# A two-layer graph network on one core: the preparation and the first layer's products in one block, instead of one after the other

## The chip, the cores and the metric

The kernel runs on one NeuronCore of a Trainium2 chip. The metric is the device time of one execution in microseconds; less is better. Engines are named as the profile names them: PE is TensorE, DVE is VectorE, ACT is ScalarE, POOL is GpSimd, SP is SyncE, which here only issues DMAs.

## The reference, cut to what matters

1,250 nodes with 768 features, 40,000 edges sorted by destination. A graph attention block (four heads of 512, then one of 768), then a graph convolution block. All matrix products are float32; the kernel makes them from two parts (hi and lo) of each operand, in three products.

```python
h = jnp.maximum(_layernorm(x, axis=-1), 0.0)
x = x + _L0_gnn_ref(h, edge_index, ...)          # two attention layers
h = jnp.maximum(_layernorm(x, axis=-1), 0.0)
x = x + _L1_gnn_ref(h, ..., edge_index)          # two graph convolutions

def _gat_layer(x, src, dst, W, a_src, a_dst, bias, concat):
    h = (x @ W).reshape(N, H, C)                 # W1: 768 x (4*512)
    al_s = jnp.einsum('nhc,hc->nh', h, a_src)
    al_d = jnp.einsum('nhc,hc->nh', h, a_dst)
    e = jax.nn.leaky_relu(al_s[src] + al_d[dst], NEG_SLOPE)
    ...softmax over the edges of a destination, weighted sum, + bias
```

## The kernel before, in words

Rows stand in `T` = 10 tiles of 128 nodes. Each block of the program (`nc.Block()`) gives every engine a queue of its own, in the order in which the code is written; engines wait for each other only through semaphores, and at the end of a block all of them meet at a barrier. There is no scheduler. `build` calls `front`, `first_layer` and `second_half`; the change touches the first two.

`front` (lines 202 to 442) does two things. **The rows:** SP loads ten tiles of `x` into `xr`; DVE takes the statistics of all ten (`row_stats`, lines 169 and 170), ACT takes the root of all ten variances at once (line 302), DVE makes `rstd` and `nmr` (lines 175 to 179 and 432); POOL normalizes tile by tile (line 293), PE turns each tile by six transposes into the PSUM tile `p_x` (line 345), ACT writes `xT_hi` with the relu (line 305) and DVE `xT_lo` (line 439). **The edges:** DVE and PE turn the sorted edges into `parts_of`, from which later the matrix of edge counts is made: `edges_in`, `chunk_windows`, `edge_keys`, `window_bounds`, `spread_chunks`, `window_parts` on DVE, `transpose_edges`, `transpose_spans`, `window_rows`, `pick_chunks` on PE. These stand between the tiles, by the two dictionaries `between`.

`first_layer` then makes the products with W1. Head after head (order 1, 2, 3, 0), tile after tile, `tile(n)` is 18 matmuls of 512 columns (six slices of the features, three hi and lo products each, line 1137); n runs to `FIRST` = 30, and ten more follow for head 0. ACT copies each product to `stage` (line 705, two slots) and SP stores it in `h_scratch` (line 641). A `stage` slot is written again only when its store has landed (`spilled`), and `tile(n)` waits until `stage` holds tile n-2. Beside this, DVE builds one-hot rows for 80 windows (`hot`, line 808, seven slots), PE counts each window with six small matmuls (line 1150) and ACT writes three windows at a time to `counts` (line 695). `windows_after(n)` gives three windows after each of the tiles 0 to 26. DVE also reduces W1 with the attention vectors (`attention_column`, line 861; four after each of the first three tiles of a head, by `columns(n)`, counted by the semaphore `v_done`). At each change of head the one copy of W1's slice, `w_st`, is split into `w_hi` (ACT, line 690) and `w_lo` (DVE, line 802).

The next head's weights overwrite `w_st`, so SP loads them only after the last use of the old ones. That wait stands in SP's queue ahead of the store of tile 6:

```python
if n in (6, 16, 22):
    j = {6: 1, 16: 2, 22: 3}[n]
    sp.wait_ge(v_done, 2 * KD * j)
    sp.wait_ge(wlo_done, KD * j)
    load_weights(sp, j)
sp.wait_ge(h_out, n + 1)
sp.dma_start(h_scratch[ORDER[i], :, n % T, :], stage[:, n % 2, :]).then_inc(spilled[n % 2], 16)
```

After tile 28 comes one more count with a dynamic number of rounds (`extra_chunks` on DVE, `count_extra` on PE; one round with these edges), which needs all windows in `counts`.

Of the kernel before, what the change touches and what calls it, by code (L numbers as in the profile page):

```python
# [83 lines left out]
class Memory:  # L84

    def __init__(self, nc, keep):
# [46 lines left out]
        self.abc = late("abc", [P, 2, HID], fp32)  # L133


def build(nc, x, src, dst, W1, as1, ad1, b1, W2, as2, ad2, b2, G1, c1, G2, c2, out):
    keep = ExitStack()
    with keep:
# [7 lines left out]
        def load_weights(sp, i):  # L146
            h = ORDER[i]
            for a, vec in enumerate((as1, ad1)):
                sp.dma_start(mem.abc[:, a, :], vec[h:h + 1, :].to_broadcast([P, HID])).then_inc(a_in, 16)
            sp.dma_start(mem.w_st[:, :, :], W1.rearrange("(k p) n -> p k n", p=P)[:, :, h * HID:(h + 1) * HID]).then_inc(w_in, 16)  # L150

        with ExitStack() as st:
            front(nc, st, mem, x, src, dst, load_weights, tile_in)
        with ExitStack() as st:
            first_layer(nc, st, mem, W2, b1, as2, ad2, h_scratch, w_in, a_in, load_weights, tile_in)
# [44 lines left out]


def front(nc, st, mem, x, src, dst, load_weights, tile_in):
    pb, sem = makers(nc, st)
    sb = Area(nc, mem.at_w, mem.at_late)
    ident, ones, pick, xT = mem.ident, mem.ones, mem.pick, mem.xT
    codes, parts_of, place, low, key = mem.codes, mem.parts_of, mem.place, mem.low, mem.key
    until, reach, total = mem.until, mem.reach, mem.total
    xr = Area(nc, mem.at_weights, mem.at_weights + T * D * 4)("xr", [P, T, D], fp32)
    stats = sb("stats", [P, T, 2, 6], fp32)
    mv = sb("mv", [P, T, 2], fp32)  # L210
    ve, root, rstd, nmr, tmp = (sb(n, [P, T], fp32) for n in ("ve", "root", "rstd", "nmr", "tmp"))
    e_i = sb("e_i", [EP, 2, EJ, EC], i32)
    e_f = sb("e_f", [EP, 2, EJ, EC], f32r)
    s_i = sb("s_i", [EC, NW * FIX], i32)
    s_hi = sb("s_hi", [EC, NW * FIX], i32)
    s_lo = sb("s_lo", [EC, NW * FIX], i32)
    d_f = sb("d_f", [EC, NW * FIX], fp32)
    sc = Area(nc, mem.at_hs, mem.at_weights)
    spread = [sc(f"spread{j}", [EP, NW, FIX], f32r) for j in range(EJ)]
    steps = sc("steps", [EP, EJ, FIX], i32)  # L220
    steps_f = sc("steps_f", [EP, EJ, FIX], fp32)
    base = sc("base", [EC, NW, FIX], i32)
    base_f = sc("base_f", [EC, NW, FIX], fp32)
    w_i = sc("w_i", [EP, 2, NW], i32)
    w_f = sc("w_f", [EP, 2, NW], fp32)
    c_i = sc("c_i", [EP, 2, EJ], i32)
    c_f = sc("c_f", [EP, 2, EJ], fp32)
    dmm = sc("dmm", [EP, 2, EJ], fp32)
    ov = sc("ov", [EP, 2, EJ, NW], fp32)
    met = sc("met", [EP, 2, EJ, NW], fp32)  # L230
    cand = sc("cand", [EP, 2, NW], fp32)
    far = sc("far", [NW, 2], fp32)
    wc = sc("wc", [NW, 3], fp32)
    tri = sc("tri", [NW, NW], fp32)
    p_x = [pb("p_x0", [P, 8, P]), pb("p_x1", [P, 8, P])]
    p_e = pb("p_e", [EC, 2, 512])
    p_w = pb("p_w", [NW, 2, EP])
    p_r = pb("p_r", [P, 3, NW])
    e_in = sem("e_in")
    made = sem("made")  # L240
    v_step = sem("v_step")
    pad_zero = sem("pad_zero")
    roots = sem("roots")
    var_done = sem("var_done")
    norm_ready = sem("norm_ready")
    h_done = sem("h_done")
    xt_done = sem("xt_done")
    hi_done = sem("hi_done")
    lo_done = sem("lo_done")
    ef_ready = sem("ef_ready")  # L250
    et_done = sem("et_done")
    spread_ready = sem("spread_ready")
    picked = sem("picked")
    red_ready = sem("red_ready")
    wt_done = sem("wt_done")
    wc_ready = sem("wc_ready")
    wr_done = sem("wr_done")

    with nc.Block() as block:
        @block.sync  # L260
        def _(sp):
            for t in range(T):
                if t == T - 1:
                    sp.wait_ge(pad_zero, 1)
                sp.dma_start(xr[0:rows_of(t), t, :], x[t * P:t * P + rows_of(t), :]).then_inc(tile_in[t], 16)
            load_weights(sp, 0)

        @block.gpsimd
        def _(pool_):
            nc.gpsimd.memset(ident[:, :], 0.0).then_inc(made, 1)  # L270
            nc.gpsimd.memset(tri[:, :], 1.0).then_inc(made, 1)
            nc.gpsimd.memset(ones[:, :].bitcast(fp32), 1.0).then_inc(made, 1)
            nc.gpsimd.memset(pick[:, :].bitcast(fp32), 0.0).then_inc(made, 1)
            for a in range(2):
                nc.gpsimd.iota(w_i[:, a, :], pattern=[[WD, NW]], base=a * (WD - 1), channel_multiplier=0).then_inc(made, 1)
            nc.gpsimd.iota(c_i[:, 0, :], pattern=[[1, EJ]], base=1, channel_multiplier=EJ).then_inc(made, 1)
            nc.gpsimd.iota(c_i[:, 1, :], pattern=[[-1, EJ]], base=NCH, channel_multiplier=-EJ).then_inc(made, 1)
            nc.gpsimd.iota(steps[:, :, :], pattern=[[1, EJ], [-1, FIX]], base=0, channel_multiplier=EJ).then_inc(made, 1)
            nc.gpsimd.iota(base[:, :, :], pattern=[[-WK, NW], [0, FIX]], base=OFFSET, channel_multiplier=0).then_inc(made, 1)
            pool_.wait_ge(made, 10)  # L280
            nc.gpsimd.affine_select(out=ident[:, :], in_=ident[:, :], compare_op=ALU.not_equal, fill=1.0,
                                    base=0, pattern=[[-1, P]], channel_multiplier=1).then_inc(made, 1)
            nc.gpsimd.affine_select(out=tri[:, :], in_=tri[:, :], compare_op=ALU.is_ge, fill=0.0,
                                    base=0, pattern=[[1, NW]], channel_multiplier=-1).then_inc(made, 1)
# [1700 lines left out]
```

## Time and profile before

| what | us |
|---|---|
| three runs: median, lowest, highest | 1232.4, 1225.87, 1234.49 |
| the profiled execution: its own time | 1236.01 |
| its span | 1234.1 |
| PE, DVE, ACT busy in the span | 1135.5, 848.9, 507.9 |

The span begins with the first instruction that the profile shows; 1.9 us of the profiled time lie around it. A busy share is an average over the whole program. For this change only the first 216 us matter, and there the order in which the queues release each other.

### The profile page before, as it was taken

How to read it: one execution, taken by the hardware profiler on the slowest of the kernel's cores; microseconds unless marked ns; L12 is line 12 of the kernel's file. 1: busy time of each engine (PE TensorE's matmuls, PEld its weight loads, DVE VectorE, ACT ScalarE, POOL GpSimd, SP SyncE). 2: the span in 40 equal slices, each digit the busy share in tenths (PEclk: the TensorE clock that was granted, in tenths of full speed). 3: DMA queues.
4: the chain of work that ended last, by engine and by line, in shares of the span. 5: the costliest groups of instructions: out<-in, count | busy, mean ns of one | idle time of the engine just before them, and what ended most of it. 6: DMA issues, size and time to landing. Idle time of an engine off the chain costs nothing. (4 is left out here: it accounts for less than half of the span.)

```text
span 1234.1 us, 17461 instructions
## 1 busy us (share of the span) xinstructions
PE 1135.5 (92%) x7119; PEld 1063.4 (86%) x7119; DVE 848.9 (69%) x1374; ACT 507.9 (41%) x1037; POOL 24.5 (2%) x39
## 2 busy tenths in 40 slices
PE   1699999997999999999999999957999899999998
PEld 1588887777999999899989999847999899889998
DVE  7897886939876888588866788578775832351263
ACT  1313233126655655466545666125445723341111
POOL 5000000002000000000000000000000000000000
PEclk9899999999999999999999999877999999999999
DMA  5023313002002010111002000004100400000311
GB/s 203 9 57 107 120 51 112 9 1 82 31 1 82 5 52 1 35 52 52 1 1 86 27 27 1 1 14 125 43 35 27 150 1 1 16 23 1 123 67 62
DMA packets 27618, 58.44 MB, mean 47 GB/s; under 512 B 3492, under 2 KB 6152, under 8 KB 27536
## 3 DMA queue, kind: packets, MB, share of 16 engines
q1 hardware_dynamic: 27344, 56.96, 14.1%
q8 instruction: 59, 0.97, 0.3%
q10 hardware_dynamic: 192, 0.32, 0.1%
q14 instruction: 23, 0.19, 0.1%
HBM read 41.73 MB, written 15.54 MB: 46 GB/s over the span
## 5 line engine op out<-in xcount | busy, mean ns | idle before, releaser
L1253 PE MATMUL banks<-hs,ring_hi 128*128 128x258 f32 (+1 forms) x1600 | 301.7, 290 | 4.0 <-DVE ring_lo L508 2.1
L1253 PEld LDWEIGHTS banks<-hs,ring_hi 128*128 128x128 f32 (+1 forms) x1600 | 250.1, 190 | 5.7 <-issue 2.5
L1253 PE MATMUL banks<-hs,ring_lo 128*128 128x258 f32 (+1 forms) x800 | 228.1, 285 | 0.0
L482 ACT ACTIVATE e<-banks,al 128x256 f32<-128x256 f32 (+1 forms) x500 | 194.0, 492 | 22.3 <-PE banks L467 22.3
L1253 PEld LDWEIGHTS banks<-hs,ring_lo 128*128 128x128 f32 (+1 forms) x800 | 151.9, 190 | 0.0
L490 ACT ACTIVATE ring_hi<-pf 128x512 fp32r<-128x512 f32 (+1 forms) x125 | 81.7, 654 | 161.5 <-DVE pf L501 158.4
L1281 PE MATMUL banks<-w_hi,oT_hi 128*128 128x384 f32 (+1 forms) x320 | 111.6, 349 | 11.3 <-DVE rows L1000 5.5
L499 DVE TENSOR_TENSOR e<-e 128x512 f32<-128x512 f32 (+1 forms) x125 | 84.6, 677 | 39.1 <-ACT e L482 38.9
L1281 PE MATMUL banks<-w_hi,oT_lo 128*128 128x384 f32 (+1 forms) x320 | 110.9, 347 | 0.0
L1281 PE MATMUL banks<-w_lo,oT_hi 128*128 128x384 f32 (+1 forms) x320 | 110.8, 346 | 0.0
L1137 PE MATMUL banks<-w_hi,xT_hi 128*128 128x512 f32 x240 | 98.6, 411 | 3.5 <-DVE w_lo L802 3.5
L1137 PE MATMUL banks<-w_hi,xT_lo 128*128 128x512 f32 x240 | 95.1, 396 | 0.0
L1137 PE MATMUL banks<-w_lo,xT_hi 128*128 128x512 f32 x240 | 94.8, 395 | 0.0
L808 DVE TENSOR_TENSOR hot<-codes,parts_of 125x1920 bf16<-125x1920 uint16 x80 | 87.0, 1151 | 9.8 <-PE banks L1150 9.8
L501 DVE SCALAR_TENSOR_TENSOR pf<-e,counts 128x512 f32<-128x512 f32 (+1 forms) x125 | 85.0, 680 | 4.3
L508 DVE TENSOR_TENSOR ring_lo<-pf,ring_hi 128x512 fp32r<-128x512 f32 (+1 forms) x125 | 84.1, 673 | 2.3 <-ACT ring_hi L490 1.7
L1832 PE MATMUL banks<-hs_hi,ring_hi 128*128 128x386 f32 x200 | 70.4, 352 | 7.8 <-DVE ring_lo L508 6.3
L1000 DVE TENSOR_TENSOR rows<-rows,banks 128x384 f32<-128x384 f32 (+1 forms) x80 | 43.9, 551 | 48.5 <-PE banks L1281 47.3
L1281 PEld LDWEIGHTS banks<-w_hi,oT_hi 128*128 128x128 f32 (+1 forms) x320 | 61.5, 192 | 13.8 <-DVE rows L1000 6.8
L1832 PE MATMUL banks<-hs_lo,ring_hi 128*128 128x386 f32 x200 | 68.8, 344 | 0.0
L1832 PE MATMUL banks<-hs_hi,ring_lo 128*128 128x386 f32 x200 | 68.6, 343 | 0.0
L1933 PE MATMUL banks<-z_hi,d_hi 128*128 128x384 f32 (+1 forms) x200 | 67.6, 338 | 0.0
(267 smaller groups left out, 2117.3 us busy)
## 6 DMA issues: line engine op xcount, KB each, us to landing
h_scratch<-stage SPq DMA_DIRECT2D x30, 256.0 KB, 2.0
hs<-h_scratch SPq DMA_DIRECT2D x30, 256.0 KB, 2.8
w_st<-in_L_gnn_W SPq DMA_DIRECT2D x4, 1536.0 KB, 10.6
w_st<-in_L_gnn_W SPq DMA_DIRECT2D x16, 384.0 KB, 3.4
gw_st<-in_L_gnn_W SPq DMA_DIRECT2D x12, 384.0 KB, 3.9
xr<-in_x SPq DMA_DIRECT2D x9, 384.0 KB, 6.9
rows<-in_x SPq DMA_DIRECT2D x9, 384.0 KB, 3.3
x_scratch<-rows SPq DMA_DIRECT2D x9, 384.0 KB
```

Of the source, the lines that this page charges most:

```text
L482: last = nc.scalar.activation(self.e[:, local % 2, a, i, 0:n], self.p_shift[:, a, 0:n], ACT.Exp, bias=scores[a][:, g * G + i:g * G + i + 1])
L490: nc.scalar.activation(self.ring[0][:, g, :, 0:n], self.pf[:, (c * NG + g) % 2, :, 0:n], ACT.Copy)\
L499: nc.vector.tensor_tensor(e[:, 0], e[:, 0], e[:, 1], ALU.max).then_inc(self.e_max, 1)
L501: nc.vector.scalar_tensor_tensor(out=self.pf[:, local % 2, :, 0:n], in0=e[:, 0], scalar=1.0, in1=counts[:, g * G:(g + 1) * G, d0:d0 + n], ...
L508: nc.vector.tensor_tensor(self.ring[1][:, g, :, 0:n], self.pf[:, (c * NG + g) % 2, :, 0:n], self.ring[0][:, g, :, 0:n].bitcast(fp32), ALU. ...
L808: nc.vector.tensor_tensor(hot[:, wd % SLOTS, :, :, :].rearrange("e a i (v t) -> e (a i) v t", t=2), codes[:, :, :, :].rearrange("e a i (v ...
L1000: nc.vector.tensor_tensor(acc, acc, p_g[i % 2][0:m, 0:HALF], ALU.add).then_inc(g_out, 1)
L1137: last = nc.tensor.matmul(p_h[n % 2], xT[a][:, k, t * P:(t + 1) * P], w[b][:, k, :], start=u == 0, stop=u == 3 * KD - 1)
L1253: last = nc.tensor.matmul(p_a[0:m, dt, half, 0:HH], wt.ring[a][:, s // G, s % G, dt * P:dt * P + m], hs[:, s, b, half * HH:(half + 1) * HH ...
L1281: last = nc.tensor.matmul(p_g[i % 2][0:m, 0:HALF], oT[a][:, k, dt * P:dt * P + m], w2[b][:, k, half * HALF:(half + 1) * HALF], start=j == ...
L1832: last = nc.tensor.matmul(p_a(t)[0:m, half, 0:AH], wt.ring[a][:, s // G, s % G, dt * P:dt * P + m], hs[b][:, s, half * AH:(half + 1) * AH] ...
L1933: last = nc.tensor.matmul(p_q(d)[0:m, half, :], d_hi[0:k, d % 2, s, 0:m], z[a][0:k, s, half * HALF:(half + 1) * HALF], start=s == 0 and a ...
```

## The change

The two blocks become one, with no barrier between them. What the queues hold in the new order:

- Statistics, roots and factors are made in three parts, tiles 0 to 2, 3 to 5 and 6 to 9 (`PARTS`), and POOL normalizes after each part.
- PE turns two tiles and the edges, then does `tile(n)` and behind it turns tile n+2. `transpose_spans`, `window_rows` and `pick_chunks` stand behind tiles 3, 4 and 6.
- SP loads W1's first slice behind the third tile of `x`. The attention vectors `abc` come behind the weights, not ahead of them, in all four loads.
- On DVE the edge steps, the columns of the first head and `xT_lo` alternate. Four conversions from integer to float are gone (`w_f`, `steps_f`, `base_f`, `c_f`); one copy of PSUM is new (`rows_of_w`).
- No window is counted before tile 9 (`FIRST_COUNT`). The 80 windows fall on tiles 9 to 27, four or five after each. At a change of head four of them stand between the six `w_lo`.
- `stage` and `junk` lie elsewhere in memory, the PSUM banks 4 to 7 are `p_x`.

The core of the diff:

```diff
-        return range(n * NW // (FIRST - 3), (n + 1) * NW // (FIRST - 3)) if n < FIRST - 3 else range(0)
+        k, tiles = n - FIRST_COUNT, FIRST - 2 - FIRST_COUNT
+        return range(k * NW // tiles, (k + 1) * NW // tiles) if 0 <= k < tiles else range(0)
...
         @block.sync
+            for t in range(T):
+                if t == T - 1:
+                    sp.wait_ge(pad_zero, 1)
+                sp.dma_start(xr[0:rows_of(t), t, :], ...).then_inc(tile_in[t], 16)
+                if t == 2:
+                    load_weights(sp, 0)
+            load_vectors(sp, 0)
             for n in range(FIRST):
                 if n in (6, 16, 22):
                     sp.wait_ge(v_done, 2 * KD * j)
                     sp.wait_ge(wlo_done, KD * j)
                     load_weights(sp, j)
+                    load_vectors(sp, j)
...
         @block.scalar
-            weight_hi(0)
+            deviations(0)
+            weight_hi(0, range(0, 3))
+            turned_hi(0)
+            weight_hi(0, range(3, KD))
+            turned_hi(1)
             for n in range(FIRST):
+                if n + 2 < T:
+                    turned_hi(n + 2)
+                if n + 1 < len(PARTS):
+                    deviations(n + 1)
                 if n % T == T - 1:
                     weight_hi(n // T + 1)
...
         @block.vector
-            weight_lo(0)
+            row_parts(range(0, 3))
+            factors(0)
+            edges_in()
+            weight_lo(0, range(0, 3))
+            turned_lo(0)
+            weight_lo(0, range(3, KD))
+            turned_lo(1)
+            row_parts(range(3, 6))
+            factors(1)
+            turned_lo(2)
+            edge_keys()
+            turned_lo(3)
+            row_parts(range(6, T))
+            factors(2)
+            turned_lo(4)
+            chunk_windows()
+            turned_lo(5)
+            window_bounds()
+            columns(0)
+            turned_lo(6)
+            spread_chunks()
+            turned_lo(7)
+            columns(1)
+            turned_lo(8)
+            window_parts()
+            turned_lo(9)
+            columns(2)
             for n in range(FIRST):
...
                 if n % T == T - 1:
-                    weight_lo(n // T + 1)
+                    soon = iter(windows_after(n + 1))
+                    for k in range(KD):
+                        weight_lo(n // T + 1, [k])
+                        if k % 2 == 0 or k == KD - 1:
+                            for wd in itertools.islice(soon, 1):
+                                count_hot(wd)
+                                ahead += 1
...
         @block.tensor
+            beside = {3: transpose_spans, 4: window_rows, 6: pick_chunks}
+            for t in range(2):
+                turn_rows(t)
+            transpose_edges()
             for n in range(FIRST):
                 tile(n)
+                if n + 2 < T:
+                    turn_rows(n + 2)
+                if n in beside:
+                    beside[n]()
                 for wd in windows_after(n):
                     count(wd)
```

Here `deviations(i)` is ACT's root of part i (it waits for DVE's `var_done`), `turned_hi(t)` and `turned_lo(t)` write `xT_hi` and `xT_lo` of tile t, `factors(i)` waits for the root, and `turn_rows(t)` waits for POOL's tile t and for `xT_lo` of tile t-2.

**Where instructions stand now.** First ACT, from its start; `root` is the root of the variances, `xT_hi` the turned tile, `stage` the copy of a product. Before:

```order
L302 ACTIVATE root<-ve 128x10 [waits var_done]
L305 ACTIVATE xT_hi<-p_x 128x6x128 [waits xt_done] x10
L259 UNCONDITIONAL_BRANCH
L680 UNCONDITIONAL_BRANCH [waits barrier_Pool_Activation_PE_DVE_SP_release]
L690 ACTIVATE w_hi<-w_st 128x512 [waits w_in]
L690 ACTIVATE w_hi<-w_st 128x512 x5
L705 ACTIVATE stage<-banks 128x512 [waits h_ready] x2
```

and in the changed kernel:

```order
L555 ACTIVATE norm_root<-norm_ve 128x3 [waits var_done]
L541 ACTIVATE w_hi<-w_st 128x512 [waits w_in]
L541 ACTIVATE w_hi<-w_st 128x512 x2
L559 ACTIVATE xT_hi<-banks 128x6x128 [waits xt_done]
L541 ACTIVATE w_hi<-w_st 128x512 [waits w_in]
L541 ACTIVATE w_hi<-w_st 128x512 x2
L559 ACTIVATE xT_hi<-banks 128x6x128 [waits xt_done] x2
L555 ACTIVATE norm_root<-norm_ve 128x3 [waits var_done]
L576 ACTIVATE stage<-banks 128x512 [waits h_ready]
L559 ACTIVATE xT_hi<-banks 128x6x128 [waits xt_done]
L555 ACTIVATE norm_root<-norm_ve 128x4 [waits var_done]
L576 ACTIVATE stage<-banks 128x512 [waits h_ready]
```

The copies of products 0 and 1 now stand behind the second and third root.

Second DVE, around the change from head 1 to head 2: `hot` is a one-hot window, `w_lo` the weights' low part, `junk,vcol` an attention column. Before, the columns of head 1 are long done there:

```order
L808 TENSOR_TENSOR hot<-codes,parts_of 125x1920 [waits hot_used] x21
L802 TENSOR_TENSOR w_lo<-w_st,w_hi 128x512 [waits whi_done] x6
L808 TENSOR_TENSOR hot<-codes,parts_of 125x1920 [waits hot_used] x3
L861 ISA junk,vcol<-w_st,abc 128x512 [waits v_done,a_in,w_in]
L861 ISA vcol 128x1
```

In the changed kernel, from the last step of the edges on:

```order
L735 TENSOR_TENSOR parts_of<-d_f,s_hi 125x80x6
L754 SCALAR_TENSOR_TENSOR xT_lo<-banks,xT_hi 128x6x128 [waits hi_done,s_step]
L819 ISA junk,vcol<-w_st,abc 128x512 [waits v_done]
...
L766 TENSOR_TENSOR hot<-codes,parts_of 125x1920 x4
L760 TENSOR_TENSOR w_lo<-w_st,w_hi 128x512 [waits whi_done]
L766 TENSOR_TENSOR hot<-codes,parts_of 125x1920
L760 TENSOR_TENSOR w_lo<-w_st,w_hi 128x512 [waits whi_done] x2
L766 TENSOR_TENSOR hot<-codes,parts_of 125x1920
```

The last four columns of the first head now come directly ahead of the first windows, behind `xT_lo` of tile 9, and only then is `v_done` at 12.

## Rows read from the trace of the kernel before

**Rows 1.** The page: busy time, share of the span, instructions

```profile
PE 1135.5 (92%) x7119; PEld 1063.4 (86%) x7119; DVE 848.9 (69%) x1374; ACT 507.9 (41%) x1037; POOL 24.5 (2%) x39
```

**Rows 2.** Windows: length, busy per engine (count), granted clock, DMA share, GB/s

```profile
10.00:20.00 10.00, 0.00 (x0) 0.00 (x0) 9.11 (x27) 0.21 (x1) 0.00 (x0) 1.00 0.97 348
20.00:30.00 10.00, 5.67 (x26) 5.30 (x26) 8.90 (x16) 2.43 (x3) 9.66 (x8) 1.00 0.00 1
...
120.00:140.00 20.00, 20.00 (x127) 16.53 (x126) 20.00 (x28) 3.19 (x7) 0.00 (x0) 1.00 0.14 53
```

**Rows 3.** Timeline of the front: start, length, instructions, idle before

```profile
9.21 0.21 DVE L170 BATCH_NORM_AGGREGATE mv<-stats 128x2 f32<-128x12 f32 x1
...
18.54 0.17 DVE L429 TENSOR_SCALAR ve<-mv 128x10 f32<-128x10 f32 x1
...
20.34 11.77 POOL L293 TENSOR_SCALAR xr<-xr,rstd,nmr 128x768 f32<-128x768 f32 x10 [14.37 <-DVE nmr L432]
...
21.82 1.51 PE L345 MATMUL p_x<-ident,xr 128*128 128x128 f32 x6 [21.82 <-POOL xr L293]
...
23.12 1.80 PE L313 MATMUL p_e<-ident,e_f 80*125 80x80 f32 x8
...
25.15 1.16 DVE L372 TENSOR_TENSOR ov<-w_f,dmm 80x320 f32<-80x320 f32 x1
...
30.66 0.94 DVE L439 SCALAR_TENSOR_TENSOR xT_lo<-p_x,xT_hi 128x768 fp32r<-128x768 f32 x1
...
42.37 0.64 PEld L345 LDWEIGHTS p_x<-ident,xr 128*128 128x128 f32 x6 [0.70 <-issue]
...
52.78 3.70 DVE L802 TENSOR_TENSOR w_lo<-w_st,w_hi 128x512 fp32r<-128x512 f32 x6 [0.97 <-ACT w_hi L690]
...
53.53 0.80 PE L1137 MATMUL banks<-w_hi,xT_hi 128*128 128x512 f32 x1 [3.55 <-DVE w_lo L802]
```

**Rows 4.** Granted clock around the first product (windows)

```profile
46.00:48.00 2.00, 0.00 (x0) 0.00 (x0) 1.97 (x4) 0.00 (x0) 0.00 (x0) 0.70 0.00 0
...
56.00:57.00 1.00, 1.00 (x4) 0.82 (x3) 1.00 (x2) 0.00 (x0) 0.00 (x0) 0.50 0.00 0
57.00:58.00 1.00, 1.00 (x5) 0.77 (x5) 1.00 (x2) 0.00 (x0) 0.00 (x0) 0.99 0.00 0
```

**Rows 5.** Groups by form, 0 to 205 us: busy, mean ns, idle before

```profile
L808 DVE TENSOR_TENSOR hot<-codes,parts_of 125x1920 bf16<-125x1920 uint16 x80 | 87.0, 1151 | 9.8 <-PE banks L1150 9.8
...
L861 DVE CUSTOM_DVE_ANT_0 junk<-w_st,abc 128x512 bf16<-128x512 f32 x48 | 30.1, 684 | 0.0
...
L305 ACT ACTIVATE xT_hi<-p_x 128x768 fp32r<-128x768 f32 x10 | 8.1, 810 | 23.8 <-PE p_x L345 23.7
```

**Rows 6.** Timeline of SP's DMA issues at tile 6

```profile
87.40 0.37 SPq L149 DMA_DIRECT2D abc<-in_L_gnn_att_src  x1
...
92.41 49.22 SPq L641 DMA_DIRECT2D h_scratch<-stage  x10
```

**Rows 7.** Landing of the stores issued from 81.5 to 125.0 us

```profile
DMA to landing us min/median/max: 2.0/2.0/7.6
```

**Rows 8.** Timeline of ACT and DVE within the products

```profile
97.22 0.60 ACT L705 ACTIVATE stage<-banks 128x512 f32<-128x512 f32 x1 [4.38 <-PE banks L1137]
...
102.65 0.60 ACT L705 ACTIVATE stage<-banks 128x512 f32<-128x512 f32 x1 [4.38 <-PE banks L1137]
...
180.60 12.90 DVE L808 TENSOR_TENSOR hot<-codes,parts_of 125x1920 bf16<-125x1920 uint16 x12
```

**Rows 9.** Timeline of the end of the thirty tiles, ACT and DVE

```profile
205.89 0.60 ACT L705 ACTIVATE stage<-banks 128x512 f32<-128x512 f32 x1 [3.79 <-PE banks L1137]
209.97 0.60 ACT L705 ACTIVATE stage<-banks 128x512 f32<-128x512 f32 x1 [3.48 <-PE banks L1137]
...
203.07 0.06 DVE L817 MEMSET round__495<- 128x1 f32 x1 [2.23 <-ACT counts L695]
...
207.08 0.26 DVE L848 TENSOR_SCALAR extra<-place,own_key 125x160 bf16<-125x160 uint16 x1
```

More of the change, by code:

```diff
@@ L554, in first_layer @@
     at_d = rest("at_d", [1, 1], i32)
+    xr = Area(nc, mem.at_weights, mem.at_x)("xr", [P, T, D], fp32)
+    e_i, e_f = mem.e_i, mem.e_f
+    stats, mv = mem.stats, mem.mv
+    ve, root, rstd, nmr, tmp = mem.norm
+    sc = Area(nc, mem.at_hs, mem.at_hs + SLOTS * 2 * FIX * WK * 2)
+    spread = [sc(f"spread{j}", [EP, NW, FIX], f32r) for j in range(EJ)]
+    s_i = sc("s_i", [EC, NW * FIX], i32)
+    s_hi = sc("s_hi", [EC, NW * FIX], i32)
+    s_lo = sc("s_lo", [EC, NW * FIX], i32)
+    d_f = sc("d_f", [EC, NW * FIX], fp32)
+    base = sc("base", [EC, NW, FIX], i32)
+    steps = sc("steps", [EP, EJ, FIX], i32)
+    w_i = sc("w_i", [EP, 2, NW], i32)
+    c_i = sc("c_i", [EP, 2, EJ], i32)
+    dmm = sc("dmm", [EP, 2, EJ], fp32)
+    ov = sc("ov", [EP, 2, EJ, NW], fp32)
+    met = sc("met", [EP, 2, EJ, NW], fp32)
+    cand = sc("cand", [EP, 2, NW], fp32)
+    far = sc("far", [NW, 2], fp32)
+    wc = sc("wc", [NW, 3], fp32)
+    tri = mem.edges("tri", [NW, NW], fp32)
+    rows_of_w = mem.edges("rows_of_w", [P, 3, NW], fp32)
     hs = Area(nc, mem.at_hs, mem.at_weights)("hs1", [P, T, 2, HA], f32r)
@@ L681, in _, with weight_hi @@
         def _(act):
-            def weight_hi(i):
+            def weight_hi(i, ks=range(KD)):
                 act.wait_ge(w_in, 16 * (i + 1))
-                for k in range(KD):
+                for k in ks:
                     if i >= 1:
@@ new lines, in spread_chunks @@
+            def spread_chunks():
+                dve.wait_ge(wr_done, 1)
+                chain(nc.vector.tensor_copy(rows_of_w[:, :, :], p_r[:, :, :]))
+                first = rows_of_w[0:EP, 0, :].unsqueeze(2).to_broadcast([EP, NW, FIX])
+                for j in range(EJ):
+                    nc.vector.tensor_tensor(spread[j][:, :, :], first, steps[:, j, :].unsqueeze(1).to_broadcast([EP, NW, FIX]),
+                                            ALU.is_equal).then_inc(spread_ready, 1)
+                chain(nc.vector.tensor_copy(until[:, :], rows_of_w[:, 2, :]), False)
+                chain(nc.vector.tensor_tensor(reach[:, :], rows_of_w[:, 1, :], rows_of_w[:, 2, :], ALU.subtract), False)
+                chain(nc.vector.tensor_scalar(total[:, :], rows_of_w[0:1, 2, NW - 1:NW], 1.0, None, ALU.max), False)
@@ new lines, in row_parts, with factors @@
+            def row_parts(tiles):
+                for t in tiles:
+                    dve.wait_ge(tile_in[t], 16)
+                    row_stats(nc, chain, stats, mv, xr, t)
+            def factors(i):
+                tiles = slice(*PARTS[i])
+                nc.vector.tensor_scalar(ve[:, tiles], mv[:, tiles, 1], EPS, None, ALU.add).then_inc(var_done, 1)
+                dve.wait_ge(roots, i + 1)
+                inverse_root(nc, chain, ve[:, tiles], root[:, tiles], rstd[:, tiles], tmp[:, tiles])
+                nc.vector.scalar_tensor_tensor(out=nmr[:, tiles], in0=mv[:, tiles, 0], scalar=-1.0, in1=rstd[:, tiles],
+                                               op0=ALU.mult, op1=ALU.mult).then_inc(norm_ready, 1)
@@ L801, in weight_lo, with turned_lo @@
+            def turned_lo(t):
+                dve.wait_ge(hi_done, t + 1)
+                hi = xT[0][:, :, t * P:(t + 1) * P].bitcast(fp32)
+                nc.vector.scalar_tensor_tensor(out=xT[1][:, :, t * P:(t + 1) * P], in0=p_x[t % 2][:, 0:KD, :], scalar=0.0,
+                                               in1=hi, op0=ALU.max, op1=ALU.subtract).then_inc(lo_done, 1)
+            def weight_lo(i, ks=range(KD)):
+                for k in ks:
                     dve.wait_ge(whi_done, i * KD + k + 1)
```

398 lines of the change are left out of this document (166 added, 232 removed).

## The prediction

> **What bounds the kernel now.** I read the page's busy times first: PE is busy 92% of the span [rows 1], so over the whole program a cut must come out of PE's idle time or its slow stretches. The windows show where the first of these lies: from 20 to 30 us DVE works 8.90 of 10 us and PE 5.67, while from 120 to 140, among the W1 products, both read 20.00 of 20 [rows 2]. The timeline gives the reason: DVE does all statistics before the first factor (18.54), POOL's first tile starts at 20.34, and the first product stands at 53.53 behind the barrier [rows 3]. The front is thus bound by DVE, the products by PE: a tile without windows takes 4.08 us (209.97 - 205.89) [rows 9] and one with three windows 5.43 (102.65 - 97.22) [rows 8], so a window costs PE 0.45. The change lays the front beside the products. Its gain is what the first product moves ahead, less what comes back as work and as waits; I follow that to the end of tile 29, 209.97 + 4.08 = 214.05 us before [rows 9]. Behind it all queues are as they were, and everything there waits for this tile.
>
> **Term 1, the start of the products.** Statistics of tile 2 are done at 9.42; root and factors take 20.34 - 18.54 = 1.8, POOL 1.18 a tile (11.77 / 10), so the first tile is normalized at 12.4. Then come two turns (1.5 and 1.3, a later one alone takes 1.51 as well) and the eight edge transposes (1.6, from 23.12 to the next turn) [rows 3]: 16.7 us. W1's slice is there by then: 3 x 0.39 + 1.57 + 0.32 MB at 348 GB/s [rows 2] is 8.8 us behind the first issues, an estimate of 12. DVE meanwhile does 2.0 us of edge conversion, three `w_lo` (0.62 each) and `xT_lo` of tile 0 (0.94) and is through at 16. First product 16.7 instead of 53.53: **36.8 us earlier**. Loads of 14 us would make it 17.5.
>
> **Term 2, tiles 0 to 9.** PE now has between the tiles what was done before them: nine tiles (0 to 8) 36.7, eight turns at the 0.64 to 0.7 of the row at 42.37 [rows 3] 5.8, the three edge steps, 18 short matmuls in the records, 4.0 at the 1.80 / 8 of the edge transposes [rows 3]: 46.5 us. Then the clock. It reads 0.70 over 46 to 48, 0.50 until 57, and 0.99 behind, after PE had idled from 44.1 and worked from 53.53 on [rows 4]; products take 0.43 instead of 0.23 there. I charge one such stretch to tile 0 and one to tile 3, 1.65 each: 3.3. Then the waits. ACT's queue has the third root ahead of `stage` 1, and that root waits for the statistics of tiles 6 to 9, which on DVE stand behind this: part 2 from 18.8 to 22.7, its root behind `xT_hi` of tile 2 (24.2), factors 25.5, `xT_lo` 2, `edge_keys` 2.7, `xT_lo` 3, four tiles of 1.3: 35.3. So `stage` 1 ends at 36.1, and tile 3, ready at 32.7, waits 3.4. `chunk_windows` (25.15 to 30.66, 5.5 us) [rows 3] ends at 43.4 and makes `transpose_spans` wait 0.8. Sum 46.5 + 3.3 + 3.4 + 0.8 = 54.0: tile 9 starts at 70.7. Before, it started at 102.65 + 1.35 = 104.0 [rows 8], with 27 windows already counted. The removed conversions and the new copy cost and give nothing: from tile 6 on DVE waits for PE's turns in this walk, 1.4 to 2.0 us each time.
>
> **Term 3, the second slice of W1.** This is where I expect the gain to go. SP may load it only when `v_done` is 12, and the last four columns now stand behind `xT_lo` of tile 9: PE's turn of tile 9 ends at 66.6, ACT 0.81, `xT_lo` 0.94, four columns of 0.61 (30.1 / 48 is 0.63) [rows 5]: 70.8. Before, they were over at 72 and the load was issued at 87.40, 22 us ahead of its use. Behind the load, in SP's queue, stands the store of tile 6, and `stage` 8 waits for its landing, `weight_hi` for `stage` 8 on ACT. In the row of before the same group was issued from 87.40 and its store (92.41) landed 7.6 later, at 100.0: 12.6 us [rows 6, 7]. With the store right behind the load I take 11.7, because it no longer waits for its own tile. Then 0.5 for `stage`, 0.55 `w_hi`, 0.62 `w_lo`: tile 10 starts at 84.2. PE is through with tile 9 and its four windows at 70.7 + 4.08 + 1.8 = 76.6, so it stands for **7.6 us**. Before, tile 10 started at 109.4 (104.0 + 4.08 + 1.35). The lead there is 25.2 us.
>
> What the load alone needs is less: 1.57 MB at the rate above is 4.5 us, and with about 2 to land 6.5; so this term lies between 2.4 (only the weights are waited for) and 8.5 (12.6).
>
> On the ordering there is a rule of the Trainium skill, page "DMA: Bandwidth & Descriptors", section "Queues, rings and completion order": descriptors are taken in ring order on each DMA engine, but completion is not first in, first out per issuing engine. By it a store could land before the load ahead of it, if it used fewer engines; the row shows the opposite here, 7.6 us against the usual 2.0 for a store of the same shape, so I keep the order. By the freer reading the sum would be 5 us better.
>
> **Term 4, tiles 10 to 29.** PE had 50 windows left here and now has 76: 26 x 0.45 = **11.7 us** more. DVE has for the stretch from tile 9 to 28: 80 windows at 12.90 / 12 = 1.075 [rows 8], 36 columns at 0.61 and twelve `w_lo`, 115 us; PE has 18 x 4.08 + 36 = 110 from tile 10 to 27. Both are full, and the seven slots of `hot` let DVE run ahead by seven windows only, so during the 7.6 us stand DVE can't use its time. Walking the two queues against each other gives: at tile 10 the four interleaved windows hold `w_lo` back (1.3), the clock is low after the stand (2.2), PE waits for `hot` in the windows of tiles 12, 13 and 23, where the columns stand ahead of them (3.1), and for `extra_chunks` 1.4: it takes 207.16 - 202.9, that is 4.3 us, from the last `counts` on [rows 9], but there is now one tile (4.08) less between. **8.0 us** in all, between 2 (DVE is ahead everywhere) and 13 (below).
>
> **The sum.** 25.2 - 11.7 - 8.0 = 5.5 us at the end of tile 29. The barrier of 1.3 us is in term 1. Against the profiled execution: 1236.0 - 5.5 = 1230.5. That execution lies 3.6 above the median shown, so for the median 1232.4 - 5.5 = **1227**. A measurement of this kernel can tell about 1%, 12 us, from no change; this is under it.
>
> **Rivals.**
> 1. *The stand at tile 10 and its echo are small.* If `stage` 8 isn't held (term 3 at 2.4), and PE's low clock and the waits of term 2 come to 3 instead of 7.5, the lead is 5.2 + 4.5 greater, and term 4 gives back perhaps 3: gain 12 to 18, 1217 us. For it: the order of SP's queue now puts the weights first. Against it: the row of the store.
> 2. *DVE becomes the bound from tile 10 on, and the gain is nil.* If a window costs DVE its mean of 1.151 [rows 5] instead of the 1.075 between starts, 80 of them take 6 us more, all on the path: 1233. For it: 115 against 110 us. Against it: twelve in 12.90.
> 3. *Slower: PE never reaches the full clock in the front.* The turns from 21.8 on took 1.51 for six, as at 0.50 later, and 0.64 at 42.37, though the clock reads 1.00 throughout [rows 3]; so a PE that stops every few microseconds can run at half speed. If tiles 0 to 8 ran so, each would take 7.7 instead of 4.1, 32 us in all, of which DVE's waits and the 3.4 us cover some 8: 24 later, a loss of 18, 1250 us. It turns into a loss when more than two further tiles (3.6 each) run at the low clock, more than the 5.5 of the sum. Against it: 18 products in a row are more work than six turns, and the clock came back within 3.5 us of them [rows 4].
> 4. *The change doesn't do what it says:* the weights or the root hold the first product to 25 or later, and then the 8 us take the whole gain: 1236.
>
> **Chances and range.** Forecast 0.60, rival 1 0.15, rival 2 0.14, rival 3 0.06, rival 4 0.05. The forecast's own bounds are 1222 to 1231. The range of 8 in 10 takes in most of rival 1 and rival 2 and the scatter of the three runs (4 us about the median): 1217 to 1236. Faster by over 1% (below 1220.1) 0.16, within 1% 0.77, slower by over 1% 0.07.
>
> **What would show it.** In the profile after: first product at 16 to 18; a wait of PE of about 3 us ahead of tile 3 with `stage` 1 behind the root; the second load of `w_st` issued at about 71; PE idle 7 to 8 us ahead of tile 10; `stage` 8 released by the DMA of `h_scratch`; waits of PE for `hot` that sum to some 3 us; the first `vr` product (L1172 before) at 210. A load issued before 65, or no idle time ahead of tile 10, would prove term 3 wrong and the time would be under 1222.

## The result: 10 us faster in the median, 7.6 us in the traces at the end of tile 29

| | before | after |
|---|---|---|
| median of six runs each, us | 1231.36 (1225.87 to 1234.49) | 1220.65 (1219.26 to 1226.89) |
| ratio, 95% interval | | 0.9917 (0.9893 to 0.9941) |
| the profiled execution, its span | 1236.01, 1234.1 | 1226.89, 1224.9 |
| start of the first product behind tile 29 | 215.74 | 208.16 |
| from there to the end of the span | 1018.4 | 1016.7 |

The ratio makes the gain 10.2 us, between 7.3 and 13.2. The forecast of 1227 is 6 us too high, of which 1 is the median of before, now taken over more runs. The traces split the difference of the two spans, 9.2 us, into two parts: 7.6 in the stretch that was changed, 1.6 behind it, where the program is the same. The point between them is the first product behind tile 29, before and after:

```profile
215.74 0.40 PE L1172 MATMUL banks<-xT_hi,v_hi 128*8 128x512 f32 x1 [1.65 <-DVE v_lo L886]
```

```profile
208.16 0.40 PE L1214 MATMUL banks<-xT_hi,v_hi 128*8 128x512 f32 x1 [1.65 <-DVE v_lo L874]
```

The page of the changed kernel, busy time of each engine as in [rows 1]:

```profile
PE 1134.4 (93%) x7119; PEld 1061.5 (87%) x7119; DVE 849.7 (69%) x1385; ACT 509.2 (42%) x1039; POOL 25.5 (2%) x39
```

The work is the same to within 2 us on every engine and the share of PE rose by one point; everything that follows is about when it waits.

The timeline of the front, after (start, length, engine, instruction, idle before), against [rows 3]:

```profile
11.40 4.65 POOL L518 TENSOR_SCALAR xr<-xr,norm_rstd,norm_nmr 128x768 f32<-128x768 f32 x3 [5.43 <-DVE norm_nmr L748]
11.78 1.67 ACT L541 ACTIVATE w_hi<-w_st 128x512 fp32r<-128x512 f32 x3 [1.77 <-DMA w_st<-in_L_gnn_W]
12.80 2.79 PE L1153 MATMUL banks<-ident,xr 128*128 128x128 f32 x12 [12.80 <-POOL xr L518]
...
16.93 0.78 PE L1170 MATMUL banks<-w_hi,xT_hi 128*128 128x512 f32 x1
```

POOL now starts at 11.40 instead of 20.34, the weights are there at 11.78, and the first product stands at 16.93 instead of 53.53. The same timeline around tile 3:

```profile
36.16 0.21 ACT L555 ACTIVATE norm_root<-norm_ve 128x4 f32<-128x4 f32 x1 [7.03 <-DVE norm_ve L745]
36.27 0.58 ACT L576 ACTIVATE stage<-banks 128x512 f32<-128x512 f32 x1
...
36.91 0.50 PE L1170 MATMUL banks<-w_hi,xT_hi 128*128 128x512 f32 x1 [3.86 <-ACT stage L576]
```

ACT idles 7.03 us for the third root, with the copy of product 1 ready behind it, and PE stands 3.86 us. The same around tile 10:

```profile
69.95 0.38 SPq L154 DMA_DIRECT2D w_st<-in_L_gnn_W  x1
...
71.44 9.81 SPq L463 DMA_DIRECT2D h_scratch<-stage  x3
80.31 0.60 ACT L576 ACTIVATE stage<-banks 128x512 f32<-128x512 f32 x1 [13.40 <-DMA h_scratch<-stage]
...
82.29 0.77 PE L1170 MATMUL banks<-w_hi,xT_hi 128*128 128x512 f32 x1 [6.87 <-DVE w_lo L760]
```

The load goes out at 69.95 (before: at 88.31, behind the row at 87.40 [rows 6]), the store of tile 6 right behind it. ACT idles 13.40 us, and what releases it last is the landing of that store (without it the same idle time is 2.85, experiment 2); until then it can write neither `stage` 8 nor, behind it, `w_hi`. PE, through at 75.42, stands 6.87. Before, the same product needs no wait:

```profile
109.05 0.47 PE L1137 MATMUL banks<-w_hi,xT_hi 128*128 128x512 f32 x1
```

The summary of PE's waits from 84 to 208.5 us, after (engine and line, for whom; us in total, times, longest):

```profile
PE banks L1183 <- DVE hot L766: 2.3, 6, 0.5
PE banks L1191 <- DVE extra L806: 1.8, 1, 1.8
```

Before, the same view of 55 to 216.5 us has neither of the two. The windows' cost on DVE is the same as in [rows 5]:

```profile
L766 DVE TENSOR_TENSOR hot<-codes,parts_of 125x1920 bf16<-125x1920 uint16 x80 | 87.0, 1147 | 3.8 <-PE banks L1183 3.8
```

### The profile page after: what moved, and what is told of

It reads as the page before. It is cut to its first block and busy times, and to the rows that moved or that the text cites. A ratio compares the mean times of both kernels' runs of the same rounds, so it can differ in the third digit from the quotient of the medians.

```text
span 1224.9 us, 17471 instructions
## 1 busy us (share of the span) xinstructions
PE 1134.4 (93%) x7119; PEld 1061.5 (87%) x7119; DVE 849.7 (69%) x1385; ACT 509.2 (42%) x1039; POOL 25.5 (2%) x39
## 5 line engine op out<-in xcount | busy, mean ns | idle before, releaser
L1323 PE MATMUL banks<-w_hi,oT_hi 128*128 128x384 f32 (+1 forms) x320 | 111.0, 347 | 11.4 <-DVE rows L994 5.5
```

What stands on the lines that cost most here:

```text
L1323: last = nc.tensor.matmul(p_g[i % 2][0:m, 0:HALF], oT[a][:, k, dt * P:dt * P + m], w2[b][:, k, half * HALF:(half + 1) * HALF], start=j == ...
```

## The experiments

Each is a text edit of the changed kernel, two of the kernel before. "Tile 29" is the start of the first product behind tile 29, "rest" the span less that: the same instructions in every kernel. The clock is the mean granted clock of the profiled execution.

| kernel | tile 29 | rest | clock | runs: median us, ratio to before |
|---|---|---|---|---|
| before | 215.74 | 1018.4 | 0.971 | |
| after | 208.16 | 1016.7 | 0.971 | 1220.65, 0.9917 |
| columns early | 197.39 | 1016.7 | 0.973 | 1216.13, 0.9881 (0.9851 to 0.9911) |
| load behind the store | 205.84 | 1015.9 | 0.975 | 1217.58, 0.9884 (0.9853 to 0.9914) |
| root behind `stage` 1 | 212.26 | 1015.8 | 0.972 | 1230.1, one run |
| before, late counts | 222.42 | 1017.2 | 0.970 | 1241.47, one run |
| dummy products in the wait | 207.49 | 1019.9 | 0.971 | 1229.38, one run |
| no interleaving | 206.78 | 1009.1 | 0.980 | 1217.94, one run |
| before, rows in parts | 217.09 | 1007.5 | 0.982 | 1226.53, one run |
| edge steps later | 197.47 | 1009.6 | 0.984 | 1209.14, 0.9836 (0.9809 to 0.9862) |
| and the load behind the store | 197.91 | 1011.8 | 0.978 | 1207.48, 0.9809 (0.9785 to 0.9833) |

The rest runs from 1007.5 to 1019.9 us, 12 us for the same instructions, as much as the whole gain; it is short where the clock is high. So a single time of one of these kernels says little, and the experiments are read by the stretch up to tile 29.

**1. Columns early.** The last eight columns stand ahead of `xT_lo` of tiles 7 and 8, so `v_done` is 12 sooner.

```diff
             spread_chunks()
+            columns(1)
             turned_lo(7)
-            columns(1)
+            columns(2)
             turned_lo(8)
             window_parts()
             turned_lo(9)
-            columns(2)
```

> The changed kernel with columns(1) and columns(2) one place earlier on DVE, ahead of xT_lo of tiles 7 and 8, where DVE waits for PE's turned tiles anyway. Theory (the second load of W1's slice is late because the last columns stand behind xT_lo of tile 9): v_done reaches 12 at about 60 us instead of 69.8, the load is issued then, PE's wait of 6.9 us ahead of tile 10 goes, and with it the low clock behind it; tile 29 ends some 9 to 10 us earlier than in the changed kernel (206.4), near 197. Rival (DVE is the bound from tile 10 on, the stand at tile 10 only gives it time to catch up): the wait goes, but PE waits for hot instead, and tile 29 ends at most 3 us earlier.

The timeline of this kernel:

```profile
58.55 0.38 SPq L154 DMA_DIRECT2D w_st<-in_L_gnn_W  x1
...
69.39 0.60 ACT L576 ACTIVATE stage<-banks 128x512 f32<-128x512 f32 x1 [3.46 <-DMA h_scratch<-stage]
```

The load is out 11.4 us earlier, `stage` 8 waits 3.46 for the store instead of 13.40, and PE's stand ahead of tile 10 is gone. Tile 29 comes 10.8 us earlier; 1.4 of this is tile 0, which ran at the full clock here, so the edit is worth 9.4. The place of the last two groups of columns on DVE, four columns each, carries the whole stand.

**2. Load behind the store.** The same wait attacked from the other end: the load stays late, but lets the store of tile 6 pass.

```diff
-                if n in (6, 16, 22):
-                    j = {6: 1, 16: 2, 22: 3}[n]
+                if n in (7, 16, 22):
+                    j = {7: 1, 16: 2, 22: 3}[n]
```

> The changed kernel with the load of W1's second slice one store later in SP's queue (at tile 7 instead of 6), so that the store of tile 6 lands without it. Theory (stage 8 waits for the store that is queued behind the load): the load is still issued at 70, but stage 8 no longer waits, ACT starts w_hi when the weights have landed, at about 76 to 77 instead of 80.8, and tile 10 starts at 77 to 78 instead of 82.3; tile 29 ends 4 to 5 us earlier. Rival (the weights themselves land as late as the store): no change, 0 to 1 us.

```profile
70.22 0.60 ACT L576 ACTIVATE stage<-banks 128x512 f32<-128x512 f32 x1 [2.85 <-PE banks L1170]
70.40 0.38 SPq L154 DMA_DIRECT2D w_st<-in_L_gnn_W  x1
...
76.86 3.23 ACT L541 ACTIVATE w_hi<-w_st 128x512 fp32r<-128x512 f32 x6 [6.05 <-DMA w_st<-in_L_gnn_W]
...
78.37 0.47 PE L1170 MATMUL banks<-w_hi,xT_hi 128*128 128x512 f32 x1 [2.49 <-DVE w_lo L760]
```

`stage` 8 no longer waits for a DMA. Now `w_hi` waits for the weights themselves, 6.5 us from issue to use, and PE stands 2.49 instead of 6.87: of the stand 4.4 us belong to the store's place in SP's queue and 2.5 to the load. The copy of product 10 comes 4.3 earlier, as expected; tile 10 starts at 78.37, a little behind the 77 to 78 named. At tile 29 only 2.3 are left instead of 4 to 5: 0.4 go between the copies of products 10 and 28, and 1.6 behind that, because after PE's wait for `extra` the granted clock was 0.72 over 198 to 200 us and 0.77 over 200 to 205; in the changed kernel it stayed at 1.00 behind the same wait.

**3. The root behind `stage` 1.** ACT's third root goes behind the copy of product 1, so that tile 3 needs no statistics of tiles 6 to 9.

```diff
-                if n + 1 < len(PARTS):
-                    deviations(n + 1)
+                if n == 0:
+                    deviations(1)
...
                 nc.scalar.activation(stage[:, n % 2, :], p_h[n % 2], ACT.Copy).then_inc(h_out, 1)
+                if n == 1:
+                    deviations(2)
```

> The changed kernel with the third root behind stage 1 on ACT. Theory (the wait is passed on): tile 3 starts at 33 instead of 36.9, but transpose_spans behind it waits for chunk_windows, which ends at 43.5 as before, so the 3.9 us come back there and tile 9 starts no earlier (69 to 71). Rival (the order on ACT costs the whole program 3.9 us): tile 9 and tile 29 come 3 to 4 us earlier.

PE's waits from 16 to 200 us, then the windows (length, busy per engine, granted clock, DMA share, GB/s) of this kernel:

```profile
PE banks L1131 <- DVE cand L691: 5.6, 1, 5.6
```

```profile
40.00:45.00 5.00, 1.17 (x6) 1.07 (x7) 4.88 (x7) 0.00 (x0) 3.23 (x3) 0.65 0.14 52
45.00:50.00 5.00, 5.00 (x17) 3.94 (x16) 3.19 (x13) 0.00 (x0) 0.00 (x0) 0.67 0.00 0
```

The wait ahead of tile 3 is gone, and `transpose_spans` waits 5.6 us for DVE instead of the 3.86 removed. Tile 3 starts at 33.18, but tile 9 at 71.95, later than the 69 to 71 expected: the stand is longer and the clock is low behind it, and the copy of product 28 comes 2.5 us later than in the changed kernel (0.4 of this is there at tile 0). Of the 4.1 at tile 29 the other 1.6 are a fall of the clock behind the wait for `extra`, as in experiment 2. DVE's list of work bounded the stretch, not ACT's order.

**4. Before, with late counts.** The kernel before with the new distribution of windows and nothing else: the price of the bunching alone.

```diff
-        return range(n * NW // (FIRST - 3), (n + 1) * NW // (FIRST - 3)) if n < FIRST - 3 else range(0)
+        k, tiles = n - 9, FIRST - 2 - 9
+        return range(k * NW // tiles, (k + 1) * NW // tiles) if 0 <= k < tiles else range(0)
```

> The kernel before with the new windows_after alone: no window before tile 9, four or five behind each of tiles 9 to 27. The work is the same. Theory (the denser counting makes DVE and PE wait for each other, seven slots of hot are too few): tile 29 ends 4 to 5 us later than in the kernel before (214.1), with waits of PE for hot. Rival (DVE keeps up): the same end within 1 us.

```profile
PE banks L1151 <- DVE hot L809: 3.0, 7, 0.6
...
PE banks L1159 <- DVE extra L849: 1.6, 1, 1.6
```

Tile 29 is 6.7 us later than before. 0.95 of this is there at the copy of tile 0: 0.4 before its first product, the rest in a longer stretch at the low clock. The other 5.7 are the bunching, somewhat more than the 4 to 5 expected: 3.0 for `hot` and 1.6 for `extra` show as waits of PE, 1.1 isn't accounted for. It is paid with no front beside the products, so the late counting costs it by itself.

**5. Dummy products in the wait.** 28 products of 512 columns, results unused, run while PE stands for tile 10: the same queues, but no fall of the clock.

```diff
                 for wd in windows_after(n):
                     count(wd)
+                if n == T - 1:
+                    pe.wait_ge(lo_done, T)
+                    for _ in range(28):
+                        nc.tensor.matmul(banks[:, 6, :], xT[0][:, 0, 0:P], xT[0][:, 0, 0:HID], start=True, stop=True)
```

> The changed kernel with 28 additional products of 512 columns (6.4 us, their result is not used) on PE behind tile 9's windows, in the time in which it waits for the second weights. Theory (the low clock behind the wait costs on top of the wait): the clock stays at full over 80 to 90 us, tile 10 takes what w_lo allows instead of 0.43 us a product, and tile 10's product is copied 1 to 2 us earlier than at 89.85. Rival (w_lo between the windows on DVE sets tile 10's pace, not the clock): within 0.5 us of it.

Behind the stand, the windows of the changed kernel and then of this one, and this one's timeline:

```profile
82.00:84.00 2.00, 1.71 (x4) 0.96 (x4) 2.00 (x4) 2.00 (x5) 0.00 (x0) 0.50 0.23 86
...
86.00:88.00 2.00, 2.00 (x6) 1.52 (x6) 2.00 (x4) 0.00 (x0) 0.00 (x0) 0.50 0.02 7
88.00:90.00 2.00, 2.00 (x13) 1.51 (x12) 2.00 (x5) 0.15 (x1) 0.00 (x0) 0.85 0.00 0
```

```profile
80.00:85.00 5.00, 3.44 (x13) 1.91 (x11) 4.24 (x6) 4.27 (x9) 0.00 (x0) 1.00 0.21 79
```

```profile
81.60 0.47 PE L1170 MATMUL banks<-w_hi,xT_hi 128*128 128x512 f32 x1 [0.75 <-DVE w_lo L760]
83.18 0.50 PE L1170 MATMUL banks<-w_hi,xT_hi 128*128 128x512 f32 x1 [0.65 <-DVE w_lo L760]
85.45 0.51 PE L1170 MATMUL banks<-w_hi,xT_hi 128*128 128x512 f32 x1 [0.61 <-DVE w_lo L760]
```

The clock falls to 0.50 in the changed kernel and stays at 1.00 here, yet from the copy of `stage` 8 to that of `stage` 10 it takes 9.17 us here and 9.54 there. A faster PE waits for `w_lo` four times, which DVE writes between the windows. Product 10 is copied at 88.78, 1.07 us earlier than in the changed kernel and so within the theory's words, but 0.70 of this is there at `stage` 8, ahead of the edit. The low clock at this place costs at most 0.4 us, not the 2.2 I charged: experiment 3, whose clock is 0.50 over 84 to 89 us, takes the same 9.17. And nothing of it is left at the copy of `stage` 28, 119.91 us behind that of `stage` 8 against 119.87.

**6. No interleaving.** The four windows go behind the last `w_lo` instead of between them.

```diff
-                        if k % 2 == 0 or k == KD - 1:
-                            for wd in itertools.islice(soon, 1):
+                        if k == KD - 1:
+                            for wd in itertools.islice(soon, 4):
```

> The changed kernel with the six w_lo of a new head in a row, no windows between them. Theory (the four windows between them cost PE nothing net, what tile 10 gains the counts behind it lose): tile 10's copy up to 1 us earlier than at 89.85, tile 29 within 0.5 us of the changed kernel. Rival (the windows between hold PE up): tile 29 some 1.3 us earlier.

From `stage` 8 to `stage` 10 it takes 8.19 us instead of 9.54, so the interleaving costs tile 10 1.35 us. From `stage` 8 to `stage` 28 it takes 120.24 instead of 119.87, and PE's waits for `hot` grow from 2.3 to 3.3: what DVE doesn't do between the `w_lo` comes back at the windows. The interleaving neither costs nor gives anything over the stretch. By the words of the expectation both figures missed: product 10 is copied 3.1 us earlier (86.76) and tile 29 comes 1.4 us earlier, as the rival had it. But 1.7 of both is an earlier `stage` 8 (78.57 against 80.31), ahead of the edit.

**7. Before, with the rows in parts.** Statistics, roots, factors and normalizing in three parts in the old block: is it the parts or the single block that brings the start forward?

```diff
-            for t in range(T):
-                dve.wait_ge(tile_in[t], 16)
-                row_stats(nc, chain, stats, mv, xr, t)
+            for i, (t0, t1) in enumerate(((0, 3), (3, 6), (6, T))):
+                for t in range(t0, t1):
+                    dve.wait_ge(tile_in[t], 16)
+                    row_stats(nc, chain, stats, mv, xr, t)
...
-            act.wait_ge(var_done, 1)
+            for i, (t0, t1) in enumerate(((0, 3), (3, 6), (6, T))):
+                act.wait_ge(var_done, i + 1)
```

> The kernel before with the rows normalized in the three parts, and nothing else. Theory (DVE bounds the front, so parts alone don't help): POOL's first tile starts at 11 to 12 instead of 20.3, DVE has two more factor chains (2.6 us) and waits less, and the first product comes within 1.5 us of 53.5. Rival (the chain through POOL and PE bounds it): the first product comes 4 us or more earlier.

A row of its timeline and one of PE's waits up to 56 us:

```profile
12.46 1.51 PE L347 MATMUL p_x<-ident,xr 128*128 128x128 f32 x6 [12.46 <-POOL xr L294]
```

```profile
PE p_e L315 <- DVE e_f L359: 10.0, 1, 10.0
```

PE turns its first tile at 12.46 instead of 21.82 and then stands 10.0 us for DVE's edge conversion; the first product is at 54.45, 0.9 later than before. The parts alone bring nothing, since DVE has the same work ahead of the barrier. Its time of 1226.53 is no gain: its rest took 1007.5 us at a clock of 0.982.

**8. Edge steps later.** The edits of experiments 1 and 3, and what that root then held up moved as well:

```diff
-            beside = {3: transpose_spans, 4: window_rows, 6: pick_chunks}
+            beside = {4: transpose_spans, 5: window_rows, 6: pick_chunks}
```

> cols_early with, besides, the third root behind stage 1 on ACT and transpose_spans and window_rows one tile later on PE (behind tiles 4 and 5). Theory (tile 3's wait of 3.9 us can be saved when the edge step behind it moves too): tile 3 starts near 33 instead of 36.9, no wait above 2 us at transpose_spans, and tile 29 ends 1 to 2 us earlier than in cols_early, since DVE from tile 10 on takes part of it back. Rival (PE's waits for the edge steps only move): within 1 us of cols_early.

The waits ahead of tile 3 and for `transpose_spans` are gone; PE shows 1.2 us of waits for `xT_lo` in their place. Tile 29 stands at 197.47, the same as with the columns alone, but tile 0 ran at the low clock here and ended 1.6 us later: the edit is worth about 1.6. The median is 7 us under that of the columns alone; the profiled executions differ by as much in their rest, so most of it is probably the clock, in code that the edit doesn't touch. Why this kernel got the high clock more often (0.984 in three of five runs) stays open.

**9. Edge steps later, and the load behind the store.** The edits of experiments 8 and 2 together.

> The kernel with the steps later and tile 0's and 1's columns early, and with the next layer's W load issued in tile 7 instead of tile 6. In the former, the load went out at 59.3 us ahead of the store of tile 6's h, and stage 8 was copied at 69.57 us, held 6.3 us by that store; PE then had 1.8 us of waits for DVE's w_lo in tile 10. Theory (the store behind the load still sets tile 10 a little): stage 8 is copied 5 to 7 us earlier, the copy of stage 10 comes 0.5 to 2 us earlier, and the p_row product starts at about 196, within 195 to 197.5 us. Rival (what paces tile 10 is DVE's w_lo between the windows, not the copy of stage 8): the copy of stage 8 is earlier, the copy of stage 10 is not, and the p_row product starts at 197.5 +- 0.5 us. A third: the load now collides with stage 9's gather and the same 6 us hold passes to stage 9, which costs 1 to 3 us. The median time differs from the former's 1209.1 by no more than the clock's scatter of some 4 us in all three.

```profile
66.11 0.60 ACT L576 ACTIVATE stage<-banks 128x512 f32<-128x512 f32 x1 [2.85 <-PE banks L1172]
...
74.25 0.50 PE L1172 MATMUL banks<-w_hi,xT_hi 128*128 128x512 f32 x1 [0.38 <-DVE w_lo L762]
```

The copy of `stage` 8 is 3.5 us earlier, not 5 to 7: without the store PE's product 8 itself ends last. The copy of `stage` 10 is 1.16 earlier and that of 28 1.19, as the theory said. Tile 29 lost it again: behind the wait for `extra` the clock fell.

```profile
192.00:194.00 2.00, 2.00 (x6) 1.54 (x5) 0.00 (x0) 1.04 (x2) 0.00 (x0) 0.50 0.00 0
```

So the product behind tile 29 starts at 197.91, 0.4 later than in experiment 8 and outside the 195 to 197.5 expected. The third reading isn't seen either: the copy of `stage` 9, at 70.66, waits for no DMA. The intervals of 8 and 9 overlap; either is faster than both given kernels, by some 20 to 24 us against before, of which the traces show 18 at tile 29.

One number joins the experiments: from the copy of `stage` 10 to that of `stage` 28 it takes 110.3 us in the changed kernel, 110.7 in experiments 1, 2, 3, 5, 8 and 9, and 112.1 in 6. What is saved ahead of tile 10 arrives at tile 28 nearly whole; the stretch between, with its windows, takes the same time whatever came before.

## Why the prediction was right, and where it wasn't

The direction held, and the median is faster by less than 1% and inside the range of 8 in 10. The size was too small: the gain forecast, 5.5 us, lies below the measured interval of 7.3 to 13.2, and 1220.65 lies below the forecast's own bounds, 1222 to 1231. Its place was right, though: at tile 29, where the forecast was worked out, the traces show 7.6. By its own steps:

- **Term 1** (first product at 16.7, measured 16.93): right, with all its parts; normalized rows, weights and turns came within 0.6 us of the walk. Experiment 7 shows that it needs the one block, not only the parts.
- **Term 2** (tile 9 at 70.7, PE through at 76.6; measured 69.5 and 75.42): the wait behind the root was 3.86 against 3.4. The two stretches at the low clock came where they were charged, at tile 0 and tile 3, with about 1.6 each. From tile 3 to tile 9 it took some 2 us less than charged. The wait for `transpose_spans` was 0.2 instead of 0.8, a turn took 0.58; the eight turns were charged 5.8, which is more than the 0.64 to 0.7 named gives, and the 0.64 was a row of weight loads (PEld), not of PE. The rest isn't separated.
- **Term 3** (stand 7.6, measured 6.87): the chain was the one named, every link of it, and experiments 1 and 2 showed both of its ends. The term that was off is the landing of the store, 11.7 behind the load's issue, measured 10.4; the two bounds, 6.5 for the weights alone (measured 6.5) and 12.6, hold it. The 12.6 counted from the issue of `abc` at 87.40; the load itself went out at 88.31, 11.7 ahead of that landing.
- **Term 4** (windows 11.7 and waits 8.0): the lead was 109.05 - 82.29 = 26.8 at tile 10 and 7.6 at tile 29, so 19.2 were given back, against 19.7 charged. The waits are 7.2 of them: tile 10 took 7.56 us from its first product to its copy instead of 4.47, which is 3.1 (charged 3.5), `hot` 2.3 (3.1), `extra` 1.8 (1.4). The split of tile 10's 3.5 was wrong: full clock gives back at most 0.4 (charged 2.2, experiment 5), `w_lo` in a row gives back 1.35 (charged 1.3, experiment 6), and the rest, some 1.3, neither edit alone gives back; the low clock and the pace of `w_lo` lie on top of each other there, and I had added them. The number of windows was off by one: `windows_after` gives two, not three, behind tile 0, so the kernel before has 29 counted when its tile 10 starts and 51 left, and 25 more are counted behind that point, not 26. At 0.45 they are 11.3; what is left of the 19.2, 0.7, isn't separated.
- **The sum** was 5.5 and came out at 7.6. The 2.1 are the 1.2 of term 2, the 0.7 of term 3 and 0.5 of term 4, less 0.35 because tile 10 of the kernel before starts at 109.05 and not at the 109.4 of the walk.
- **Left out** was the rest of the program, which I took as unchanged. It is, instruction by instruction, and still ran 1.6 us shorter in the profiled execution. The windows show it as low clock that fell elsewhere, first before, then after:

```profile
222.00:232.00 10.00, 10.00 (x61) 7.24 (x60) 9.72 (x10) 1.56 (x3) 0.00 (x0) 1.00 0.00 0
...
783.00:798.00 15.00, 11.95 (x74) 11.75 (x73) 7.55 (x11) 0.80 (x2) 0.00 (x0) 0.77 0.00 1
```

```profile
222.00:232.00 10.00, 10.00 (x47) 8.25 (x46) 7.87 (x11) 2.47 (x3) 0.00 (x0) 0.83 0.01 2
...
783.00:798.00 15.00, 13.42 (x82) 12.99 (x81) 5.73 (x11) 2.83 (x6) 0.00 (x0) 0.94 0.00 0
```

Whether the change makes such stretches rarer on average, or the runs drew them so, isn't settled; the 10.2 of the medians and the 7.6 of the traces differ by less than the interval's half width, 3 us.

**The rivals.** The first (no stand at tile 10) didn't happen, though the median lies between its 1217 and the forecast; it is what experiment 1 makes of the kernel, and there it does give the larger gain, 18.35 us at tile 29. The second needed 1.151 us per window on the path; PE's waits for `hot` of 2.3 us exclude it. The third, a PE that never reaches the full clock in the front, appeared for eight products of tile 0 and as many of tile 3 only. The fourth is excluded by the row at 16.93.

## What to carry to other kernels

A gain at the front of a program is worth what is left at the last point where queues meet: here 36.6 us at the first product, 26.8 at tile 10, 7.6 at tile 29, and one place on DVE, the last columns behind the wrong neighbours, cost more (9.4) than the net gain. When a load waits in an issuing queue, look at what stands behind it in that queue and who waits for that to land. Compare traces at a meeting point, with the same code on either side of it, before believing a difference of medians under 1%.

## What the runs showed of the hardware

**A store behind a load.** The store of 256 KB usually lands in 2.0 us [rows 7]. Issued right behind the 1.5 MB load it let `stage` 8 start 10.4 us after the load's issue, against 6.5 for the load itself in experiment 2.

**The granted clock at the start.** After (its two rows and its window), the first products stand 0.43 us apart for 3.5 us, although the granted clock reads 1.00; in experiment 1 they stand 0.23 apart from the first on. The timelines show every third:

```profile
18.36 0.63 PE L1170 MATMUL banks<-w_hi,xT_hi 128*128 128x512 f32 x1
19.64 0.63 PE L1170 MATMUL banks<-w_hi,xT_hi 128*128 128x512 f32 x1
```

```profile
16.00:18.00 2.00, 2.00 (x9) 1.81 (x9) 2.00 (x5) 1.42 (x3) 0.05 (x1) 1.00 1.06 347
```

```profile
17.45 0.40 PE L1170 MATMUL banks<-w_hi,xT_hi 128*128 128x512 f32 x1
18.15 0.39 PE L1170 MATMUL banks<-w_hi,xT_hi 128*128 128x512 f32 x1
```

At the start of these spans the distance of the products tells the level, not the clock's column. Of the eight kernels with this front, whose queues are the same up to there, five start tile 0 at the low level and three (experiments 1, 5 and 6) at the full one; the edge transposes ahead of it already differ, 1.81 us for eight against 1.30 to 1.58. That the same code starts at either level agrees with the Trainium skill, page "TensorE: Matmul & The Clock Gate", section "What's actually happening", by which the chip's watch on PE's activity runs freely and isn't started anew by a kernel; the two first products here lie at 16.93 and 16.68.

**The clock after short waits.** Behind one and the same wait of 1.8 us for `extra` the granted clock stayed at 1.00 in the changed kernel and in experiments 1 and 8, and fell in 2 (0.72 and 0.77), 3 and 9 (0.50 over two microseconds in each). From the copy of product 28 to the first product behind tile 29 it is 7.97 or 7.98 us in the changed kernel and in experiments 1, 5, 6 and 8, and 9.58 to 9.61 in 2, 3 and 9, with nothing between. The 12 us of scatter in the rest go with the mean granted clock, so such falls probably make them; no experiment shows it.

**DVE beside POOL.** `edge_keys`' `s_hi`, one integer instruction of 125x320, took 1.07 us while POOL normalized and 0.33 before, when POOL had nothing to do. After, then before:

```profile
27.80 1.07 DVE L699 TENSOR_SCALAR s_hi<-s_i 125x320 int32<-125x320 int32 x1
```

```profile
32.85 0.33 DVE L388 TENSOR_SCALAR s_hi<-s_i 125x320 int32<-125x320 int32 x1
```

DVE shows no idle time from there to the statistics that the third root waits for, at 35.96, so the 0.7 us lie on the way to PE's wait of 3.86 ahead of tile 3 (an estimate from these two rows). That POOL is the reason is argued from the two rows, not shown by an experiment.
